# Where VectorE keeps the row-sum denominators of an mLSTM cell: from a spare corner of PSUM to a small SBUF tile

## What is computed

```python
def cell(q, k, v):                       # for each sequence
    ig, fg = (concat(q, k, v) @ igate_w.T + igate_b).T, (concat(q, k, v) @ fgate_w.T + fgate_b).T
    cs = cumsum(log_sigmoid(fg), axis=1)
    log_D = where(tril, cs[:, :, None] - cs[:, None, :], -inf) + ig[:, None, :]
    max_log_D = max(log_D, axis=-1)
    C = (qh @ kh.T / sqrt(32)) * exp(log_D - max_log_D)
    normalizer = maximum(abs(C.sum(axis=-1)), exp(-max_log_D))
    h = (C / (normalizer + 1e-6)) @ vh
    return layernorm(h) * ln_scale

x = x + tanh(g_xattn) * cell(layernorm(x), ctx, ctx)
y = square(relu(layernorm(x) @ W_fc.T)) @ W_proj.T
x = x + tanh(g_ffn) * (spikes of 5 steps of the neuron fed with y) / 5
```

## Time and profile before

| | us |
|---|---|
| median of 3 runs | 667.49 |
| lowest and highest | 665.35, 668.03 |
| the profiled execution's own time | 667.49 |
| its span, first to last instruction | 665.7 |
| busy in the span: TensorE, VectorE, ScalarE, GpSimd | 595.0, 534.2, 488.8, 486.8 |

### The profile page before, as it was taken

The page is one execution under the profiler, slowest core; times in us unless marked ns, Lnnn a source line. Parts: engine busy times, 40 slices in busy tenths (PEclk is TensorE's granted clock), DMA queues, the critical chain, the costliest instruction groups (busy, mean ns, idle before and its releaser), DMA issues.

```text
span 665.7 us, 17636 instructions
## 1 busy us (share of the span) xinstructions
PE 595.0 (89%) x6032; PEld 489.8 (74%) x6032; DVE 534.2 (80%) x1218; ACT 488.8 (73%) x1014; POOL 486.8 (73%) x535
## 2 busy tenths in 40 slices
PE   1364788889999999999999999999999999999795
PEld 0253677778787887888788878887888877787684
DVE  5567658887988999899989898889989888958432
ACT  5565447878877888788787887888778877676563
POOL 5374477869698878977997879796988778675332
PEclk9995579989999999999999999999999999999999
DMA  6575452882369165845485527825590545300001
GB/s 199 125 197 111 83 97 67 143 163 61 86 117 227 30 132 124 179 67 96 116 177 128 94 70 164 190 52 110 118 221 19 111 99 130 82 2 32 1 32 33
DMA packets 73192, 71.33 MB, mean 107 GB/s; under 512 B 8720, under 2 KB 68752, under 8 KB 73104
## 3 DMA queue, kind: packets, MB, share of 16 engines
q1 hardware_dynamic: 71984, 70.02, 48.0%
q10 hardware_dynamic: 1120, 0.18, 0.3%
HBM read 27.44 MB, written 8.39 MB: 54 GB/s over the span
## 4 chain that ended last, share of the span: by engine, by line
PE 58%; issue 14%; POOL 10%; ACT 9%; DVE 7%; DMA 0%; POOLq 0%; ACTq 0%; DVEq 0%
PE y_ps L1050 18%; PE z_ps L990 17%; PE arg_ps L695 4%; POOL sq_lo L1033 3%; PE qk_ps L710 3%; PE misc_ps L463 3%; PE misc_ps L529 3%; DVE spikes L1068 2%; POOL c_lo L739 2%; PE pv_ps L834 2%; PE pv_ps L759 2%; POOL am_rest L637 2%; PE pv_ps L757 2%; PE pv_ps L758 1%; ACT sq_hi L1012 1%
## 5 line engine op out<-in xcount | busy, mean ns | idle before, releaser
L1033 POOL TENSOR_TENSOR sq_lo<-w_raw,sq_hi 128x512 fp32r<-128x512 f32 (+1 forms) x96 | 112.8, 1176 | 66.4 <-ACT w_raw L1013 66.3
L739 POOL TENSOR_TENSOR c_lo<-decay 128x512 bf16<-128x512 f32 x128 | 132.1, 1040 | 10.5 <-DVE decay L729 10.3
L990 PE MATMUL z_ps<-x_hi,wfc_hi 128*128 128x512 f32 (+1 forms) x288 | 117.1, 406 | 5.3 <-ACT relu L1000 2.5
L1050 PE MATMUL y_ps<-sq_hi,wpr_hi 128*128 128x512 f32 (+1 forms) x288 | 115.7, 402 | 0.9 <-POOL sq_lo L1033 0.6
L990 PE MATMUL z_ps<-x_hi,wfc_lo 128*128 128x512 f32 (+1 forms) x288 | 108.1, 375 | 0.0
L990 PE MATMUL z_ps<-x_lo,wfc_hi 128*128 128x512 f32 (+1 forms) x288 | 108.0, 375 | 0.0
L1050 PE MATMUL y_ps<-sq_lo,wpr_hi 128*128 128x512 f32 (+1 forms) x288 | 107.3, 373 | 0.0
L1050 PE MATMUL y_ps<-sq_hi,wpr_lo 128*128 128x512 f32 (+1 forms) x288 | 107.1, 372 | 0.0
L729 DVE TENSOR_TENSOR decay<-qk_ps,decay 128x512 f32<-128x512 f32 x128 | 87.0, 680 | 23.9 <-PE qk_ps L710 19.2
L721 ACT ACTIVATE decay<-arg_ps,lqk_col 128x512 f32<-128x512 f32 x128 | 86.5, 676 | 25.8 <-PE arg_ps L698 25.0
L1033 POOL TENSOR_TENSOR sq_lo<-relu,sq_hi 128x512 fp32r<-128x512 f32 (+1 forms) x48 | 56.1, 1170 | 44.5 <-ACT relu L1013 41.8
(11 more groups left out here) (138 smaller groups left out, 1688.9 us busy)
## 6 DMA issues: line engine op xcount, KB each, us to landing
x_in<-x SPq DMA_DIRECT2D x32, 256.0 KB, 3.0
v_in<-ctx_rows SPq DMA_DIRECT2D x32, 256.0 KB, 3.5
kT_in<-ctx_cols SPq DMA_DIRECT2D x32, 256.0 KB, 4.1
k_stack<-kT_hi SPq DMA_DIRECT2D x64, 128.0 KB, 3.3
k_stack<-kT_lo SPq DMA_DIRECT2D x64, 128.0 KB, 3.6
q_stack<-qT_hi SPq DMA_DIRECT2D x64, 128.0 KB, 3.9
q_stack<-qT_lo SPq DMA_DIRECT2D x64, 128.0 KB, 4.1
out<-w_raw SPq DMA_DIRECT2D x32, 256.0 KB, 3.5
```

The costliest lines, as they stand in the source:

```text
L739: e.tensor_tensor(c_lo[i % NCH][:, :], c, top(c), ALU.subtract).then_inc(sem("c_lo"), 1)
L990: ins = e.matmul(z_ps[:, tokens(q)], lhsT, rhs, start=(n == 0), stop=(n == len(terms) - 1))
L1033: e.tensor_tensor(sq_lo[n % NSQ][:, tokens(q)], relu[n % NRE][:, tokens(q)], sq_hi[n % NSQ][:, tokens(q)].bitcast(fp32), ALU.subtract).the ...
L1050: ins = e.matmul(y[:, c, :], w[:, j, c * P:(c + 1) * P], h, start=(j == 0 and i == 0 and (c == 0 or whole)), stop=(j == FT - 1 and i == 2) ...
```

## The change

The PSUM corner is given up. `denom` becomes an SBUF tile of 128 x 2 x 8 and takes over the part of `most` as well. The four small steps stay four, each with its wait, in the same order and at the same place in VectorE's queue. What differs is where they read and write:

| line | step | inputs before | output before | inputs after | output after |
|---|---|---|---|---|---|
| 852 | scalar_tensor_tensor | PSUM, SBUF | SBUF | PSUM, SBUF | SBUF |
| 853 | tensor_tensor, maximum | PSUM, SBUF | PSUM | SBUF, PSUM | SBUF |
| 854 | tensor_scalar, + 1e-6 | PSUM | PSUM | SBUF | SBUF |
| 855 | reciprocal | PSUM | SBUF | SBUF | SBUF |

In the changed kernel the four stand two lines higher, at 850 to 853. No instruction is added, removed or moved on any engine.

```diff
-        most = sb("most", [P, ST, NH], fp32)
+        denom = sb("denom", [P, ST, NH], fp32)
         rdenom = sb("rdenom", [P, ST, NH], fp32)
...
-        SPARE = NH * VW + HPC * VW
-        denom = pv_ps[:, :, SPARE:SPARE + NH]
...
             row_sum, least = pv_heads[:, :, :, DH], floor[g % 3][:, 0:ST, row:row + NH]
-            link(e, "vector", e.scalar_tensor_tensor(most[:, :, :], row_sum, -1.0, least, ALU.mult, ALU.max))
-            link(e, "vector", e.tensor_tensor(denom, row_sum, most[:, :, :], ALU.max))
-            link(e, "vector", e.tensor_scalar(denom, denom, EPS, None, ALU.add))
-            link(e, "vector", e.reciprocal(rdenom[:, :, :], denom))
+            link(e, "vector", e.scalar_tensor_tensor(denom[:, :, :], row_sum, -1.0, least, ALU.mult, ALU.max))
+            link(e, "vector", e.tensor_tensor(denom[:, :, :], denom[:, :, :], row_sum, ALU.max))
+            link(e, "vector", e.tensor_scalar(denom[:, :, :], denom[:, :, :], EPS, None, ALU.add))
+            link(e, "vector", e.reciprocal(rdenom[:, :, :], denom[:, :, :]))
```

## The result

The changed kernel is slower, by more than a measurement of it is uncertain: 673.22 us in the median of 22 runs (670.33 to 676.63) against 667.62 of the kernel before (22 runs, 664.72 to 674.98). The ratio is 1.0081, with a 95% interval of 1.0065 to 1.0096, some 5.4 us.

What follows compares the result with a forecast made beforehand. TensorE was taken to set the pace, busy 70.53 of 70.90 us a turn. 667.49 plus 0 to 0.5 for the turns and 0 to 0.5 for start and tail gave 668.0 us in the middle, range 665.6 to 672.5.

Steps and rivals of the forecast that it cites:

- the lock: SBUF port pair shared by VectorE and GpSimd: line 854 would wait until GpSimd's current instruction ends, 0.02 to 0.07 us after it.
- The steps without a wait: Lines 852 to 855 undisturbed: an h_norm changes by -48 to +28 ns, taken as zero.
- The first place of a turn: First h_norm of a loop turn, at 261.33: line 854 gets in between GpSimd's 434 and 456, no wait, 60 against 40.
- rival (a): First h_norm waits for GpSimd's 456: +0.93 us on VectorE, 0.4 on TensorE a turn, 669.5 to 670 in all; chance 0.20.
- The second, third and fourth place: Later h_norms of a turn: +0.15 to +0.20 us, covered by idle time; +0.07 to +0.12, reaching TensorE; no wait.
- It absorbs most of the 0.1: TensorE's own 0.27 us wait at 315.08 takes most of the third h_norm's 0.1, leaving 0 to 0.5 us over five turns.
- The start and the tail: The other 12 h_norms: mean wait 0.3 us, some 3.5 us on VectorE, 0 to 0.5 us counted on the span.
- (b): Fourth h_norm slips behind GpSimd's 1033, waiting some 1.1 us; about 0.5 reach TensorE a turn; 672.5 with (a); chance 0.12.
- (c): The reciprocal, line 855, takes the lock too: some 1.5 us in a turn, 676 in all; chance 0.07.
- (d): Four steps faster, or no lock for so small a step: under 1 us gained in all, 667.0; chance 0.11.
- the race: At the first h_norm of a turn, whether line 854 or GpSimd's 456 goes first after 434; losing means some 0.93 us.
- the cover at the start: VectorE's waits at the start are hidden, as TensorE itself waits for transposes; 0 to 0.5 us for start and tail together.

Runs made afterwards that it cites:

- the pair of the table: One profile of the kernel before and the third of the unaltered changed kernel, their TensorE clocks almost alike: spans 665.7 and 671.2 us.
- the two memsets: Kernel before, but sequences 10, 14 to 30 use the SBUF tile, with two one-column memsets before the 1e-6 addition: 672.59 us against 668.33, ratio 1.0062.

## Why the prediction was wrong

**What bounds the kernel, and the lock.** Right. TensorE sets the pace, and the step that the change puts wholly into SBUF waits for GpSimd's running instruction. The experiment in which it writes PSUM shows it by itself. The prediction named the wrong section of the page for the rule of the Trainium skill: in "SBUF — State Buffer" it stands in the section on the two separate sides. With its exclusive lock the runs agree, with the 1.12 us of this step beside GpSimd's 454.

**The steps without a wait.** 851 has 171 ns (174 forecast), 852 174 (162 to 218), 853 253 (237 to 257). An undisturbed `h_norm` is 23 ns shorter, within -48 to +28. No run shows a gain from it by itself.

**The first place of a turn.** Wrong, and it is the first term of the error. "I take no wait, at 60 against 40": the step lost there in five of five turns, in each of the four profiles. The step of the reasoning that failed is "wherever it arrives during the first". It compared the step's start with the end of 434, where the start of 456 decides, and the earlier trace rows had both: 456 starts at 261.29, 0.04 us ahead of line 854. The 8 ns that line 853 saves were too few to turn that round; 454 still starts 0.02 to 0.04 us ahead of the step in every turn. Line 374 says nothing else: where it gets in between two GpSimd instructions it starts ahead of the second. The size that rival (a) gave, 0.93 on VectorE and 0.4 on TensorE, is what came: 0.94 and 0.41. This alone would have made 669.5.

**The second, third and fourth place.** Right: 0.35, 0.26 and 0.17 us, where 0.33 to 0.38, 0.25 to 0.30 and no wait had been expected. But "It absorbs most of the 0.1" did not come true: the 0.09 us by which the step at the third place is longer are found in the turn, 0.1 of its 0.5 us. That is 0.5 us over five turns, the upper end of what was counted.

**The start and the tail.** Wrong in size, the second term. The sum of the waits on VectorE over both, some 3.2 us, is near the 3.5 forecast, and so their mean over the 12 is the 0.3 that I took. But 1.7 of it fell on three places in a row, at 117, 130 and 151 us, with 0.41, 0.75 and 0.58 us over the old 0.18. What failed is "where at the start it is not the bound": the start lost 1.0 to 1.7 us there, not 0 to 0.5, and 0.33% when it was tried alone. VectorE was busy only 84% of that stretch, but TensorE stood behind `q_lo` there. In the kernel before a row says so, which I had not weighed, TensorE at the end of the start waiting for 492, and its answer in the changed kernel, waiting longer:

```profile
135.59 0.17 PE L529 MATMUL misc_ps<-gw_hi,qT_hi 128*128 128x16 bf16 x1 [1.69 <-DVE qT_lo L492]
```

```profile
134.32 0.17 PE L527 MATMUL misc_ps<-gw_hi,qT_hi 128*128 128x16 bf16 x1 [2.42 <-DVE qT_lo L490]
```

The 0.73 us between them match the wait of the step at 130 us, 0.75 over the old 0.18:

```profile
129.98 0.93 DVE L852 TENSOR_SCALAR denom<-denom 128x16 f32<-128x16 f32 x1
...
129.71 1.16 POOL L432 TENSOR_TENSOR kT_lo<-kT_in,kT_hi 128x512 bf16<-128x512 f32 x1
```

The tail lost 0.6 us in the pair of the table, where 0.5 was counted at most for start and tail together, but the kernels with the corner spread over as much among themselves.

**The rivals.** (a) happened, with its own price, but on top of a start that was priced too low. (b) did not happen in the changed kernel; forced by the two memsets, it costs 1.0 us in a turn and not 0.5; the scan at 611 took over the wait of 615. (c) did not happen: the reciprocal in SBUF stays at 252 to 256 ns next to any instruction of GpSimd. By the Trainium skill ("Vector Engine (DVE) Microarchitecture Reference", section 5.1), which does not list it among the two-port instructions, the trace agrees. (d) is refuted for the lock; its shorter steps are real, 23 ns over the four. The 62 cycles of the Trainium skill ("VectorE: DVE Perf Modes", TRN2 errata) for each of two steps would have been 130 ns, as an estimate from the page; the two steps that it names lost 8 and 4.

**The chances.** 0.22 on slower was too little. The two things that could go wrong, the race and the cover at the start, both pointed to slower, and no rival had them together. First and third place with 2.5, the start with 1.2 and the tail with 0.6 on top of 667.49 make 671.8, which is inside the range. What took the median to 673.22 and out of it is the last 1 us or so, whose cause stays open.

## What to carry to other kernels

Before moving an operand of a small VectorE step into SBUF, ask whether input and output are then both in SBUF while GpSimd is busy. The tensor_scalar here then cost what was left of GpSimd's instruction, however small it was; the reciprocal did not. Writing to PSUM was enough to avoid it. Fusing such a step into a neighbour that has a PSUM operand gave the tile without the lock, and saved an instruction. Where two engines meet within some 0.1 us, compare start with start and not start with end, take the worse case into the sum, and price a start or tail by the wait that ends last there and not by the busy share.

## What the runs showed of the hardware

Between a VectorE step and GpSimd's next instruction the earlier start goes first, in every row of every profile where the addition works on the tile. At the first place of the changed kernel GpSimd's start is 0.02 to 0.04 us ahead and the step waits for the whole instruction; at the fourth the step's start is 0.03 to 0.07 us ahead and it does not. A held step of 16 elements ended 0.02 to 0.04 us behind GpSimd's end.

A scan on VectorE with its two inputs in SBUF (line 611) is held too, 1.67 us in place of 0.68, where GpSimd's subtraction starts first (at 311.53, the scan at 311.96). Whoever starts first holds the other: in the earlier trace rows it was GpSimd that took 1.51 us behind line 612, where 1.27 to 1.31 are usual.

The long stretch at half clock in the start was 0, 27.3, 37.5 and 23.9 us in the four profiles of the changed kernel alone, so it is nothing of the change. With the corner in the start the first mark lies at 168.5 us with 37.5 us of it, 167.1 with 27.3, 166.1 with 23.9 and 166.4 with none, so spans of single profiles are best compared where it is the same.
